# A two-layer graph network on one core: part of the value scaling of the last chunk on VectorE, and the second layer's index table split in two

## The reference, cut to what matters

```python
# layer 1, graph attention with 4 heads of 64
e   = einsum('ehd,ehd->eh', q[src], k[dst]) / 8
ex  = exp(e - segment_max(e, dst)[dst])
agg = segment_sum(ex / segment_sum(ex, dst)[dst] * v[src], dst)
rst = prelu(layernorm(gate(skip, agg)))
x   = x + rst
# layer 2, weighted mean of the neighbours
h   = relu(layernorm(x))
x   = x + concat(segment_sum(h[src] * w, dst) / deg, h) @ W.T + b
```

## Time and profile before

| what | us |
|---|---|
| median of three runs | 1379.87 |
| the profiled execution, its own time | 1385.02 |
| its span, first to last instruction | 1383.2 |
| mean granted TensorE clock, share of full speed | 0.864 |

### The profile page before, as it was taken

How to read it: one execution, slowest core, us unless ns; L and a number is a source line. 1 busy time by engine, 2 the same in 40 slices (tenths; PEclk the granted TensorE clock), 3 DMA queues, 4 the chain that set the end, 5 groups by cost and what they waited for, 6 DMA issues and landing times. The chain is left out here.

```text
span 1383.2 us, 19581 instructions
## 1 busy us (share of the span) xinstructions
PE 1058.0 (76%) x4178; PEld 743.4 (54%) x4178; DVE 1037.8 (75%) x2552; ACT 609.6 (44%) x2300; POOL 830.7 (60%) x889
## 2 busy tenths in 40 slices
PE   7989599999999999999982076657666877666674
PEld 4434367777777777777761054435443554444443
DVE  4545589999999999999977983647656765666574
ACT  2111279989989989899895562000000000000000
POOL 3000677777777777777720003777777777777774
PEclk9999889999999999999996578877887677777686
DMA  7111677777777777777750012333333333333335
GB/s 191 38 53 69 178 206 208 203 211 207 207 207 209 205 209 207 207 207 206 210 171 23 0 50 91 107 104 106 103 106 105 105 107 104 107 103 107 104 112 156
DMA packets 75379, 194.01 MB, mean 140 GB/s; under 512 B 15682, under 2 KB 30050, under 8 KB 75268
## 3 DMA queue, kind: packets, MB, share of 16 engines
q0 software_dynamic: 55680, 170.57, 43.1%
q1 hardware_dynamic: 16078, 18.99, 4.2%
q10 hardware_dynamic: 3510, 3.20, 0.7%
HBM read 179.66 MB, written 13.03 MB: 139 GB/s over the span
## 5 line engine op out<-in xcount | busy, mean ns | idle before, releaser
L633 POOL DMA_INDIRECT ring<-qv_tab,v_src x440 | 424.5, 965 | 261.3 <-POOLq L205 125.7
L1264 POOL DMA_INDIRECT y_ring<-y_tab,e_idx x416 | 395.3, 950 | 271.8 <-POOLq L1014 145.3
L694 ACT ACTIVATE ring<-ring 128x64 f32<-128x64 f32 x1760 | 439.6, 334 | 0.0
L1326 PE MATMUL bank<-y_ring,hot 128*128 x880 | 301.6, 490 | 160.0 <-SPq L1272 146.9
L1354 DVE SCALAR_TENSOR_TENSOR kx<-bank,rdeg,kx 128x256 f32 x440 | 212.9, 484 | 193.8 <-PE bank L1326 183.5
L1326 PEld LDWEIGHTS bank<-y_ring,hot 128*128 128x128 f32 x880 | 197.7, 242 | 252.7 <-issue 223.7
L740 PE MATMUL bank<-kx,hotT 128*128 x880 | 238.9, 396 | 43.2 <-ACT hotT L651 43.2
L749 PE MATMUL bank<-ring,hot 128*128 128x261 f32 x880 | 259.5, 394 | 3.5 <-ACT ring L694 3.5
L1280 ACT COPY ownT<-bank 128x256 f32<-128x256 f32 x25 | 9.3, 372 | 489.7 <-PE bank L1299 489.7
L740 PEld LDWEIGHTS bank<-kx,hotT 128*128 128x128 f32 x880 | 162.8, 193 | 98.4 <-issue 78.2
L917 DVE TENSOR_TENSOR acc<-acc,bank 128x261 f32 x440 | 184.0, 418 | 16.0 <-PE bank L749 11.9
(11 more groups left out here) (220 smaller groups left out, 779.3 us busy)
## 6 DMA issues: line engine op xcount, KB each, us to landing
ring<-qv_tab,v_src POOLq DMA_INDIRECT x440, 3.7
y_ring<-y_tab,e_idx POOLq DMA_INDIRECT x416, 2.8
qv_tab<-qv_out SPq DMA_DIRECT2D x25, 256.0 KB, 2.0
y_tab<-y_out SPq DMA_DIRECT2D x12, 256.0 KB, 2.1
out_dram<-kx ACTq DMA_DIRECT2D x24, 128.0 KB
xs<-in_x_dram SPq DMA_DIRECT2D x4, 640.0 KB, 14.4
kx<-in_x_dram SPq DMA_DIRECT2D x4, 640.0 KB
xs<-in_x_dram SPq DMA_DIRECT2D x1, 512.0 KB
```

Of the source, the lines that this page charges most:

```text
L633: pool.indirect_dma_start(one_step(r, 0, 2 * D), None, qv_tab, bass.IndirectOffsetOnAxis(ap=v_src[:, r:r + 1], axis=0)).then_inc(got[r % R ...
L694: A.activation(part, part, ACT.Copy, scale=one_step(r, EX + h, EX + h + 1)).then_inc(scaled, 1)
L1264: pool.indirect_dma_start(y_ring[:, e % RH, :], None, y_tab, bass.IndirectOffsetOnAxis(ap=e_idx[:, e:e + 1], axis=0)).then_inc(y_got[e % R ...
L1326: T_.matmul(bank[r % SB][:, 0:D], hot[:, r % HR, :], y_ring[:, bass.ds(places[r % LOADED], 1), :], start=True, stop=True).then_inc(sums_do ...
```

## The change

Two parts.

First layer: for the last five groups (105 to 109) ScalarE scales only the first and second step of each group. The third and fourth are scaled by VectorE, one TENSOR_TENSOR of 128x256 with the four exponentials broadcast over their heads, just before the additions of the group before. A second semaphore counts these.

Second layer: `e_steps` is replaced by two tables of 440 words, places and counts, and every 20 steps TensorE's sequencer loads 20 words from each, in two TENSOR_LOADs in place of one of 30 words.

```diff
-        e_steps = sb("e_steps", [1, STEPS // LOADED, LOADED + LOADED // 2], I32)
+        e_place = sb("e_place", [1, STEPS], I32)
+        e_count = sb("e_count", [1, STEPS], I32)
...
-                    by_load = r_row[0:1, :].rearrange("o (l s) -> o l s", s=LOADED)
-                    V.tensor_scalar(e_steps[:, :, LOADED:], by_load[:, :, 1::2], 1.0, None, ALU.add)
-                    f(V.tensor_copy(e_steps[:, :, 0:LOADED], by_load))
-                    V.tensor_scalar(e_steps[:, :, 0:LOADED], e_steps[:, :, 0:LOADED], RH - 1, None, ALU.bitwise_and)
+                    V.tensor_scalar(e_count[:, :], r_row[0:1, :], 1.0, None, ALU.add)
+                    f(V.tensor_copy(e_place[:, :], r_row[0:1, :]))
+                    V.tensor_scalar(e_place[:, :], e_place[:, :], RH - 1, None, ALU.bitwise_and)
...
+            scaled_late = sem("v_scaled_late")
+            SHARED = GR - PER
...
-                        scale_v(v, 2)
-                        scale_v(v, 3)
+                        if v < SHARED:
+                            scale_v(v, 2)
+                        if v < SHARED:
+                            scale_v(v, 3)
...
-                    pe.wait_ge(scaled, (r + 1) * HEADS)
+                    if g < SHARED:
+                        pe.wait_ge(scaled, (r + 1) * HEADS)
+                    elif u < 2:
+                        pe.wait_ge(scaled, (SHARED * Q + (g - SHARED) * 2 + u + 1) * HEADS)
+                    else:
+                        pe.wait_ge(scaled_late, (g - SHARED) * 2 + u - 1)
...
+                def scale_late(g, u):
+                    r = g * Q + u
+                    dve.wait_ge(ex_ready, g + 1)
+                    dve.wait_ge(got[r % RS // 2], (r // RS + 1) * 32)
+                    v_rows = one_step(r, D, 2 * D).rearrange("p (h d) -> p h d", h=HEADS)
+                    V.tensor_tensor(v_rows, v_rows, one_step(r, EX, EX + HEADS).unsqueeze(2).to_broadcast([P, HEADS, DH]), ALU.mult).then_inc(scaled_late, 1)
...
+                    if SHARED <= v + 1 < GR:
+                        scale_late(v + 1, 2)
+                        scale_late(v + 1, 3)
                     if v > 0 and v % PER == 0:
                         tiles = coming
                         fade_open(v // PER, tiles[0])
...
-                        _, loaded = nc.values_load_multi_w_load_instructions(e_steps[0:1, r // LOADED, :], engines=[pe.engine], min_val=0, max_val=ET,
-                                                                             skip_runtime_bounds_check_because='places by RH, then counts of edge tiles')
-                        places = [p.with_bounds(min_val=0, max_val=RH - 1) for p in loaded[0:LOADED]]
-                        counts = [c & 1023 for c in loaded[LOADED:]]
+                        _, places = nc.values_load_multi_w_load_instructions(e_place[0:1, bass.ds(r, LOADED)], engines=[pe.engine],
+                                                                             min_val=0, max_val=RH - 1, skip_runtime_bounds_check_because='a remainder by RH')
+                        _, counts = nc.values_load_multi_w_load_instructions(e_count[0:1, bass.ds(r, LOADED)], engines=[pe.engine],
+                                                                             min_val=1, max_val=ET, skip_runtime_bounds_check_because='one more than the edge tile of a step')
...
-                        pe.wait_ge(landed, counts[r % LOADED // 2])
+                        pe.wait_ge(landed, counts[r % LOADED + 1] & 1023)
```

## The result

The changed kernel takes 1376.42 us (median of 17 runs, 1374.41 to 1378.17) against 1379.54 for the one before (17 runs, 1376.75 to 1381.94): a ratio of 0.9979, 95% interval 0.9973 to 0.9986, so 1.9 to 3.7 us faster. The forecast was 5.0 us less, its range 1373.0 to 1378.6. The direction and the range hold; the size is outside the interval of this measurement. By the medians it is 3.1 us less, and 1376.42 lies 0.6 above the 1374.4 to 1375.8 that the forecast gave for its own case.

A forecast was written before the change was run, and what follows sets the result against it. ScalarE's scaling was taken to bound the first layer's tail, TensorE's last register load the second's end. Terms 0.1 - 1.5 - 3.6 = -5.0 us took the median from 1379.87 to 1374.9 us, range 1373.0 to 1378.6.

The forecast's parts named there:

- The last load holds up the second layer's end, whatever name the wait has: Second layer's end: TensorE's 12.59 us load for step 420, not SyncE, delays the last 20 steps.
- Rows off a multiple of 16 bytes go word by word: TensorE's register loads: misaligned rows cost 0.236 us a word; aligned rows go in pieces of four words.
- A contended load of 20 words takes 2.53: Second layer's end: each new last load beside ScalarE's stores takes 2.53 us, bounds 1.36 and 6.9.
- rival 2: Last loads: contention is paid per load, two of 6.9 us; net -0.3, 1379.6 us; chance 0.07.
- The landing bounds next, 1.7 or 2.4 us before the last addition: Second layer's end: TensorE catches up, the last gather's landing bounds; last addition 1.7 to 2.4 us behind its signal.
- 3.6 us: Second layer's end: gain from the split table, taken between 3.9 and 3.2 us.
- The first tail gives 1.5 us, since VectorE's additions take over: First layer's end: last addition at 734.73 instead of 736.26, VectorE's addition chain bounding instead of ScalarE.
- rival 1: Second layer's end: last load already hidden without a profiler; only -1.4 left, 1378.5 us; chance 0.14.
- rival 3: First layer's end: TensorE at 1.2 GHz, 0.9 us a step, bounds; net -2.5, 1377.4 us; chance 0.07.
- rival 4: Second layer's loads: a new table begins off a multiple of 16, each load 4.7 us; 1382.5 us; chance 0.06.
- The table in the projection costs 0.1: Projection: the strided 220-element add becomes one of 440, 0.1 us more on VectorE before the selection matrices.
- The sum: Whole kernel: 0.1 - 1.5 - 3.6 = -5.0 us, carried from the profile to the median, 1374.9 us.

The follow-up runs named there:

- both experiments: Kernel before, table rows lengthened to 32 words with 30 loaded: ratio 0.9977; changed kernel, both new tables begun 8 bytes later: 1386.88 us, ratio 1.0053 to before.
- the tables alone: Kernel before with only the second part, two tables of 20-word rows, all scaling left on ScalarE: 1376.31 us, ratio 0.9969.
- interleaving: Changed kernel, one late multiplication before a group's first addition, the other between first and second: 1372.62 us, ratio to before 0.9944.
- padded rows: Kernel before, its one table kept, rows 32 words long with 30 loaded: 1375.57 us, ratio 0.9977.
- stores last: Kernel before, ScalarE issuing no store until all 440 additions are done: one run, 1388.73 us.
- the second batch: Changed kernel unaltered, timed again beside its two halves on one chip, against the kernel before: 1375.59 us, ratio 0.9967.

## Why the prediction came out as it did, point by point

- *The last load holds up the second layer's end, whatever name the wait has.* Right. It was put down to SyncE; padding the rows, splitting the table or holding back the stores each took the wait away.
- *Rows off a multiple of 16 bytes go word by word.* Right as far as the start of the row goes, by both experiments (tested 8 bytes off, no other distance). That the load goes in words or in pieces of four is a reading; two lengths fit it: 20 words 4.74, 30 words 7.09, so 0.235 a word. Aligned, 20 words are five pieces of four, 1.36, or 0.27 each; 30 are seven pieces and two words, 7 x 0.27 + 2 x 0.235 = 2.36, which is what they take.
- *A contended load of 20 words takes 2.53.* 2.52 and 3.06; 2.75 and 2.18 in the second profile. The bound of 6.9 for an excess paid per load (rival 2) falls: TensorE's aligned loads of five pieces pay 0.7 to 1.7 us more, 20 single words 3.5 and 3.6, 30 single words 5.3 to 5.6. The excess grows with the length of the load: 7.09 to 12.6, 4.74 to 8.3 and 2.36 to 4.26 are all a factor of about 1.8.
- *The landing bounds next, 1.7 or 2.4 us before the last addition.* Right: from the last signal to the last addition's start it is 1.73 us in the tables alone and in both profiles of the changed kernel, 2.39 with interleaving, padded rows and stores last; the difference is TensorE's clock in the last two steps. **3.6 us** was a little small: in the changed kernel's profiles the second tail is 4.0 to 4.5 us shorter, with interleaving 3.6 to 4.1.
- *The first tail gives 1.5 us, since VectorE's additions take over.* 1.33 to 1.46 in four profiles. A pair cost 0.37, priced 0.38. Two smaller errors cancel in it: in the changed kernel's profile the first addition of the chunk stood 0.2 us earlier than forecast, and one gap of 0.99 without a multiplication (727.50 to 728.49) added 0.35. The forecast had called such a gap a sign of being wrong; it stands once in each of the five profiles with the scaling part, and what makes it was not found.
- *Hidden anyway, when nobody profiles* (rival 1). Falls: the tables alone give 2.5 to 5.9 us in the timing, and the load was 12.67 and 12.38 us long in two more executions. The timed runs carry a span and a clock in the record as well, so an effect that recording has on all of them alike is not excluded.
- *TensorE's clock bounds the first tail* (rival 3). It did not; the additions kept their 0.64 but for the one gap named above.
- *Slower if misaligned* (rival 4). The mechanism is real and the case did not arise. Its price was too low: the second tail grew by 6.1 to 6.6 us, not by 2.4 to 4.2. The loads themselves took 16.6 us in place of 12.6, 4.0 more, near the 4.2 of the upper of my two prices. Most of the rest is a late start: the load began 16.6 us before the last gather in place of 19.0 and 18.8, since TensorE had not made up for the 9.5 us of the pair before. I had taken the earlier loads as hidden at any length. The 1382.5 given for this rival also lies at the upper end of what its own terms add up to, 1380.9 to 1382.7.
- *The table in the projection costs 0.1.* Right: from the start of the `r_row` subtraction to the start of the selection matrices it is 1.64 us (32.59 to 34.23) in place of 1.54 (35.12 to 36.66).
- **The sum.** This is where the forecast was off: 5.0 us forecast, 3.1 measured. The two tails less the 0.1 add to 5.3 to 5.9 us in the profiles, and the second batch agrees with 5.0 (0.9967, 3.0 to 6.1 us less); the first and larger one does not (1.9 to 3.7). The step at fault is the one that carried a difference of tails over to the median one for one. Between the tails lies a stage whose length is not fixed, and the forecast put nothing down for it. From the last addition of the first layer to the first gather of the second it took 111.6, 108.9, 109.3, 109.0 and 109.0 us in the five profiles without the scaling part, and 111.9, 111.8, 111.4, 108.4 and 108.5 in the five with it. TensorE's products for `y_tab` (L1221) show what differs; in the last group, in the kernel before, first the profile with 111.6, then the one with 108.9:

```profile
L1221 PE MATMUL bank<-w1T,hT x28: 379/379/634, 835.4 to 843.6; 128*128 128x256 f32 x28
```

```profile
L1221 PE MATMUL bank<-w1T,hT x28: 379/379/483, 832.6 to 839.9; 128*128 128x256 f32 x28
```

The same holds for a stretch of that stage by its granted clock, again first the one and then the other:

```profile
832.00:842.00 10.00, 7.90 (x35) 0.83 0.19 66
```

```profile
832.00:842.00 10.00, 7.61 (x37) 1.00 0.19 67
```

Some of those matmuls ran at 1.2 GHz and took 0.63 in place of 0.38. All ten profiles go with this: in the stretch from 90 to 100 us after the last addition the granted clock was 0.84 in the four long ones and 1.00 in the six short ones. The long ones take 2.1 to 3.5 us more. That the clock makes up the whole of it was not tested. Three of five executions with the scaling part and one of five without were of the long kind. If that is more than chance, moving the stage by 1.5 us also moves where the clock falls in it, and gives back about 1 us: the gap would be half explained. Ten profiles cannot tell, and it stays open. So does what else differs between the two batches.

## What to carry to other kernels

A load of a table row into registers stops the sequencer until it is done: start every row on a multiple of 16 bytes (30 words took 2.36 us there and 7.09 when 8 bytes off), pad it if need be, and look at the last load of a loop, which no slack follows. When an engine waits "for" a signal that came long before, look at its sequencer's own queue for a load. When work moves to an engine that is in a chain of dependent instructions, put each piece into one of the gaps of the chain: side by side a pair cost 0.37 us, in two gaps 0.08.

## What the runs showed of the hardware that I had not expected

- Stores issued on another queue lengthen register loads: 7.09 to between 12.4 and 12.7 us (30 words, 8 bytes off), 4.74 to 8.2 and 8.4 (20 words, 8 bytes off), from 1.36 to between 2.0 and 3.5 (20 words aligned), 2.36 to 4.26 (30 words aligned), and none of it when the stores come later.
- The same code gave 1379 us on some chips and 1650 on one, and a change worth 0.2% on the former may be worth 1% on the latter: padded rows, 0.9977 and 0.9892. The slower chip's gathers, when nothing held them, kept the same 1.25 us; its TensorE and VectorE paused.
